# Narrow experts whose weighted rows are scattered, adding, into four sums in DRAM, in place of gathers by token

## What is computed

```python
x = x + xattn0(layernorm(x), ctx, mask)      # a0: 16 heads
x = x + ffn0(layernorm(x))                   # m0: 64 experts, top 8, 128 rows each
x = x + xattn1(layernorm(x), ctx, key_mask)  # a1: one head
x = x + local_ffn(layernorm(x))              # two layers of windowed attention
x = x + xattn2(...); x = x + ffn2(...)       # a2, m2: 8 experts, top 2
x = x + xattn3(...); x = x + ffn3(...)       # a3, m3: 8 experts, top 2
```

```python
x_buf = zeros((E * C + 1, D)).at[idx].set(x[tok])       # E=64, C=128, D=256, K=8
h = silu(einsum(xb, w_gate)) * einsum(xb, w_up)          # F=192
y = einsum(h, w_down).reshape(E * C, -1)
contrib = y[safe] * (flat_w * valid)[:, None]
routed = segment_sum(contrib, tok, num_segments=T)
return routed + silu(x @ gate_s) * (x @ up_s) @ ws_down  # the shared expert
```

## Time and profile before

| | us |
|---|---|
| median of three runs | 2786.64 |
| the profiled execution | 2789.22 |
| its span | 2787.4 |
| PE busy | 2337.7 (84%) |
| DVE busy | 1242.1 (45%) |
| ACT busy | 1077.8 (39%) |
| POOL busy | 609.0 (22%) |

### The profile page before, as it was taken

How to read it: one execution, slowest core, us unless ns; L and a number is a source line. 1 busy time by engine, 2 the same in 40 slices (tenths; PEclk the granted TensorE clock), 3 DMA queues, 4 the chain that set the end, 5 groups by cost and what they waited for, 6 DMA issues and landing times. The chain is left out here.

```text
span 2787.4 us, 44673 instructions
## 1 busy us (share of the span) xinstructions
PE 2337.7 (84%) x13238; PEld 1707.2 (61%) x13239; DVE 1242.1 (45%) x3611; ACT 1077.8 (39%) x3675; POOL 609.0 (22%) x638
## 2 busy tenths in 40 slices
PE   5998997944789989899989799379996997099991
PEld 3774786622466745566745466269984665099991
DVE  3775332435567742477733344422222564322223
ACT  2542232421356641266631355123332554044340
POOL 3277213771121210021210000310001220400004
PEclk8988898655699999999999899689998998599995
DMA  9100796333030020000000500411015101401113
GB/s 340 73 12 29 270 355 226 94 99 89 15 133 10 9 53 0 32 11 10 9 4 1 209 0 0 155 34 32 29 32 190 67 12 48 141 31 38 34 36 96
DMA packets 141735, 213.20 MB, mean 76 GB/s; under 512 B 36220, under 2 KB 110988, under 8 KB 140409
## 3 DMA queue, kind: packets, MB, share of 16 engines
q1 hardware_dynamic: 112328, 149.90, 16.3%
q0 software_dynamic: 29264, 61.54, 6.5%
HBM read 150.69 MB, written 83.52 MB: 84 GB/s over the span
## 5 line engine op out<-in xcount | busy, mean ns | idle before, releaser
L2343 POOL TENSOR_TENSOR la_invnorm<-la_clamped,all_minushalf 128x16 f32<-128x16 f32 x32 | 92.9, 2903 | 532.4 <-DVE la_clamped L2412 532.4
L826 PE MATMUL a_score_bank<-a_fold,a_xnt 128*128 (+3 forms) x448 | 183.5, 537 | 0.0
L853 PE MATMUL a_out_bank<-a_vw,a_probst 128*128 (+5 forms) x672 | 169.9, 406 | 3.6 <-ACT a_probst L762 3.4
L745 ACT ACTIVATE a_probs<-a_score_bank,a_mx 128x77 f32<-128x77 f32 x528 | 162.1, 364 | 2.7 <-DVE a_mx L640 1.7
L2070 ACT ACT_TABLE_LOAD x40 | 51.3, 1283 | 287.5 <-PE m3e_h_bank L2043 152.3
L2043 PE MATMUL m2e_h_bank<-m2e_xt,m2e_w1e 128*128 128x108 f32 x1280 | 152.2, 278 | 0.1
L2043 PE MATMUL m3e_h_bank<-m3e_xt,m3e_w1e 128*128 128x128 f32 x1280 | 152.1, 278 | 0.1
L2494 ACT ACTIVATE la_probs<-la_probs,la_nb,la_invnorm 128x256 f32<-128x256 f32 x256 | 150.1, 589 | 5.1 <-DVE la_nb L2434 5.1
L2043 PEld LDWEIGHTS m2e_h_bank<-m2e_xt,m2e_w1e 128*128 128x128 f32 x1280 | 148.8, 195 | 0.5 <-DVE m2e_xt L2084 0.4
L2043 PEld LDWEIGHTS m3e_h_bank<-m3e_xt,m3e_w1e 128*128 128x128 f32 x1280 | 148.7, 195 | 0.5 <-DVE m3e_xt L2084 0.5
L853 PEld LDWEIGHTS a_out_bank<-a_vw,a_probst 128*128 128x128 f32 (+2 forms) x672 | 129.7, 200 | 28.2 <-issue 6.8
(11 more groups left out here) (443 smaller groups left out, 4748.1 us busy)
## 6 DMA issues: line engine op xcount, KB each, us to landing
m0w_wgu<-in_m_gu SPq DMA_DIRECT2D x32, 768.0 KB, 7.2
m_xbuf<-all_zeros POOLq DMA_DIRECT2D x36, 512.0 KB, 17.9
m_w<-in_m_w SPq DMA_DIRECT2D x16, 1024.0 KB, 12.5
m0e_wd<-in_m_down SPq DMA_DIRECT2D x32, 384.0 KB, 8.0
m_xbuf<-all_zeros POOLq DMA_DIRECT2D x20, 432.0 KB, 10.1
m0w_xb<-m_xbuf SPq DMA_DIRECT2D x32, 256.0 KB, 8.4
m_ybuf<-m0e_y POOLq DMA_DIRECT2D x32, 256.0 KB, 6.3
m2w_w<-in_m_w SPq DMA_DIRECT2D x8, 1024.0 KB
```

Source lines behind the costliest of these rows:

```text
L745: last = nc.scalar.activation(probs[u][:, h * J:(h + 1) * J], score_ps[g][:, (h - h0) * J:(h - h0 + 1) * J], ACT.Exp, bias=mx[u][:, h:h + ...
L826: last = nc.tensor.matmul(score_ps[g][:, (hs[0] - h0) * J:(hs[-1] + 1 - h0) * J].rearrange("p (h j) -> p h j", j=J), xn_t[u][:, c, :], fol ...
L853: last = nc.tensor.matmul(out_ps[:, 0:D], probs_t[u][0:n, c, :], vw[0:n, bass.ds(b, 1), c, :].rearrange("p o n -> p (o n)"), start=False, ...
L2343: nc.gpsimd.tensor_tensor(inv_norm[t % 2][:, :], clamped[t % 2][:, :], k.minus_half[:, :], ALU.pow).then_inc(powered.sem, 1)
```

## The change

In a0 each row that POOL scatters into `xbuf` becomes 288 numbers wide (it was 256): behind the 256 values stand the token's eight expert numbers, its eight weights and its own number. So DVE and ACT make each tile's weights before that tile's scatter (`rank_shift`, `soften`, `carry`), and the weight work at the end of the stage goes. POOL also fills four buffers of 2560 rows in DRAM, the sums, with zeros (16 more transfers of 512 KB), and SP stores `x` with the shared expert in the first of them.

In m0 DVE finds in each pair's rows the weight and the token (`find`, `found_at`), multiplies `y` by the weight while it copies it out of PSUM, and POOL sends each expert's 128 rows by an indirect transfer that adds to the sum's rows. The two experts of a pair go to different sums, and the next pair uses the other two, so that a sum is used again two pairs later, after a wait for its last transfer (`summed`). At the end two transfers add two of the sums to the other two. The gathers and the adding on DVE go; the fold keeps its block (`fold_stage`).

`norm_scales` ahead of a1 goes, and a1's loop gets two steps more of lag: SP loads two sums' rows for each tile, DVE adds them into `x` and makes mean and variance (`combine_before`), POOL the scale (`scale_sum`). `local.load_first` stands behind SP's last load of sums.

```diff
@@ -996,12 +1031,20 @@
                 ahead.wait_scattered(sp)
                 for q in range(len(ahead.xb)):
                     ahead.load_rows(sp, q)
+                sp.wait_ge(ahead.sum_zeroed, 16 * 16)
+                for p in range(T // 2):
+                    sp.wait_ge(shared_added, p + 1)
+                    sp.dma_start(ahead.sums[0][1 + 2 * p * P:1 + 2 * (p + 1) * P, :].rearrange("(t p) d -> p t d", p=P),
+                                 k.x[:, 2 * p:2 * p + 2, :]).then_inc(ahead.x_stored, 16)
...
+                for i, total in enumerate(ahead.sums):
+                    for c in range(0 if i else SUM_ROWS // 512 - 1, SUM_ROWS // 512):
+                        pool.dma_start(total[c * 512:(c + 1) * 512, :].rearrange("(p a) d -> p (a d)", p=P), k.zeros[:, 0:4 * D]).then_inc(ahead.sum_zeroed, 16)
...
                 def scatter(t):
                     pool.wait_ge(placed, t + 1)
+                    pool.wait_ge(weighing, 2 * (t + 1))
                     for i in range(K):
...
+                def rank_shift(t):
+                    dve.wait_ge(ranked, 5 * t + 1)
+                    if t >= 2:
+                        dve.wait_ge(softened, t - 1)
+                    nc.vector.tensor_scalar(shifted[t % 2][:, :], ahead.top[:, t, 0:K], ahead.top[:, t, 0:1], None, ALU.subtract).then_inc(shifting, 1)
+
+                def carry(t):
+
+                    dve.wait_ge(softened, t + 1)
+                    nc.vector.reciprocal(sum_top[t % 2][:, :], sum_top[t % 2][:, :]).then_inc(weighing, 1)
+                    nc.vector.tensor_scalar(ahead.rows[t % R][:, IDS], idxf[t % 3][:, :], 1.0, None, ALU.add)
+                    nc.vector.tensor_copy(ahead.rows[t % R][:, TOKEN], k.token[:, t:t + 1])
+                    dve.wait_ge(weighing, 2 * t + 1)
+                    nc.vector.tensor_scalar(ahead.rows[t % R][:, WEIGHTS], exped_top[t % 2][:, :], sum_top[t % 2][:, 0:1], None, ALU.mult).then_inc(weighing, 1)
 
```

```diff
@@ -1854,6 +1915,7 @@
 
                 def load_x(q):
                     sp.wait_ge(turned, q - NX + 1)
+                    sp.wait_ge(found, 2 * (q - NX + 1))
                     r.ahead.load_rows(sp, q)
 
...
 
             @block.gpsimd
             def _(pool):
+                pool.wait_ge(r.ahead.x_stored, 16 * (T // 2))
                 for q in range(npair):
                     pool.wait_ge(y_copied, q + 1)
-                    pool.dma_start(r.ybuf[q * 2 * P:(q + 1) * 2 * P, :].rearrange("(i p) d -> p i d", p=P), y[q % 2][:, :, :]).then_inc(stored[q % 2], 16)
-                for u in range(2):
-                    pool.wait_ge(stored[u], 16 * (npair // 2))
+                    for i in range(2):
+                        j = 2 * (q % 2) + i
+                        if q >= 2:
+                            pool.wait_ge(summed[j], 16 * (q // 2))
+                        nc.gpsimd.indirect_dma_start(sums[j][:, :], bass.IndirectOffsetOnAxis(dest[q % NY][:, i:i + 1], 0), y[q % NY][:, i, :], None,
+                                                     bounds_check=SUM_ROWS - 1, oob_is_err=True, compute_op=ALU.add).then_inc(summed[j], 16)
+                for i in range(2):
+                    for j in (i, i + 2):
+                        pool.wait_ge(summed[j], 16 * (npair // 2))
+                    pool.dma_start(sums[i][1:1 + T * P, :], sums[i + 2][1:1 + T * P, :], max_dma_last_dim=4096, accum_op=ALU.add).then_inc(r.ahead.sums_joined, 16)
...
+                def find(q):
+
+                    rows = xb[q % NX]
...
+                    if q >= 1:
+                        dve.wait_ge(found, 2 * q)
+                    for i in range(2):
+                        nc.vector.scalar_tensor_tensor(picked[:, i, :], rows[:, i, IDS], float(2 * q + i + 1), rows[:, i, WEIGHTS],
+                                                       ALU.is_equal, ALU.mult)
+                    nc.vector.scalar_tensor_tensor(spot[:, :], rows[:, :, TOKEN].rearrange("p i o -> p (i o)"), 0.0, k.spare[:, :],
+                                                   ALU.is_equal, ALU.mult).then_inc(finding, 1)
+
+                def found_at(q):
+                    rows = xb[q % NX]
+                    dve.wait_ge(finding, q + 1)
+                    if q >= NY:
+                        for i in range(2):
+                            dve.wait_ge(summed[2 * (q % 2) + i], 16 * ((q - NY) // 2 + 1))
+                    nc.vector.tensor_reduce(weight[q % NY][:, :], picked[:, :, :], AX, ALU.add).then_inc(found, 1)
+                    nc.vector.tensor_tensor(dest[q % NY][:, :], spot[:, :], rows[:, :, TOKEN].rearrange("p i o -> p (i o)"), ALU.add).then_inc(found, 1)
+
                 def copy_y(q):
                     dve.wait_ge(y_made, q + 1)
-                    if q >= 2:
-                        dve.wait_ge(stored[q % 2], 16 * (q // 2))
+                    dve.wait_ge(found, 2 * (q + 1))
                     for i in range(2):
-                        last = nc.vector.tensor_copy(y[q % 2][:, i, :], y_ps[i][:, 0:D])
+                        last = nc.vector.tensor_scalar(y[q % NY][:, i, :], y_ps[i][:, 0:D], weight[q % NY][:, i:i + 1], None, ALU.mult)
                     last.then_inc(y_copied, 1)
 
                 for step in range(npair + 3):
+                    if 2 <= step < npair + 2:
+                        find(step - 2)
                     if step >= 3:
                         copy_y(step - 3)
+                    if 2 <= step < npair + 2:
+                        found_at(step - 2)
                     if 1 <= step <= npair:
                         hide(step - 1)
         r.old_sems.close()
+
```

```diff
+                if summing:
+                    sp.wait_ge(before.ahead.sums_joined, 32)
+
+                    def load_sums(t, u):
+                        sp.wait_ge(combined.sem, combined.at(t - 2, "x"))
+                        for i in range(2):
+                            sp.dma_start(got[u][:, i, :], before.ahead.sums[i][bass.ds(t * P + 1, P), :]).then_inc(gathered[u], 16)
+                    pipeline(sp, T, (0, load_sums))
                 if local:
                     local.load_first(sp)
...
+                    if summing:
+                        nc.vector.tensor_tensor(row(k.x, t), got[u][:, 0, :], got[u][:, 1, :], ALU.add).then_inc(combined.sem, 1)
+                    else:
+                        for i in range(K):
+                            if i:
+                                done("0")
+                            nc.vector.scalar_tensor_tensor(row(k.x, t), got[u][:, i, :], before.weights[:, bass.ts(t, 1), i], row(k.x, t),
+                                                           ALU.mult, ALU.add).then_inc(combined.sem, 1)
+                    done("x")
                     nc.vector.bn_stats(row(k.stats, t), row(k.x, t)).then_inc(combined.sem, 1)
                     done("stats")
                     stand_alone(dve, before_waited)
...
+            if summing:
+                @block.gpsimd
+                def _(pool):
+                    pool.sem_inc(scaled_before.sem, 2)
+
+                    def scale_sum(t, u):
+                        pool.wait_ge(combined.sem, combined.at(t, "eps"))
+                        nc.gpsimd.tensor_tensor(col(k.rstd, t), col(k.var, t), k.minus_half[:, 0:1], ALU.pow).then_inc(scaled_before.sem, 1)
+                    pipeline(pool, T, (1, scale_sum))
```

More of the change, by code:

```diff
@@ L524, in attention @@
             routed, logged = s.steps("routed"), s.steps("logged")
+        summing = before is not None and before.m is M0
         if before:
-            K = before.m.top
+            K = 2
             got, slot = s.pair("got", [P, K, D]), s.pair("slot", [P, K], U32)
@@ L532, in attention @@
             indexed, scaled_before = s.steps("indexed"), s.steps("scaledbefore")
-            combined = s.steps("combined", *(f"{i}" for i in range(K)), "stats", "copy", "aggr", "mean", "eps")
+            combined = s.steps("combined", *(("x",) if summing else ("0", "x")), "stats", "copy", "aggr", "mean", "eps")
         def later(*phases):
@@ L1031, in _ @@
                 nc.vector.memset(none3[:, :], 0.0)
+                for rows in ahead.rows:
+                    nc.vector.memset(rows[:, D:PAYLOAD], 0.0)
                 nc.vector.tensor_copy(before16[:, :], k.before[:, :])
```

106 lines of the change are left out of this document (62 added, 44 removed).

## The result

The changed kernel takes 2802.93 us (median of 4 runs, 2798.62 to 2804.36), the kernel before beside it 2786.06: a ratio of 1.0056 (95% interval 1.0038 to 1.0073), 16 to 17 us slower. The forecast was 2778.4, 8 us faster. A second comparison, later and with 6 runs, gave 2798.3 against 2786.5, 1.0042 (1.0026 to 1.0058).

What follows compares the result with a forecast made beforehand. It took PE to set m0's pair period with DMA nearly full, and gathers to set the fold stage's end. -46.2 + 21 + 8 + 5 + 2 + 2 = -8.2, giving 2778.4 against the median; range 2760 to 2822.

Steps and rivals of the forecast that it cites:

- the join: End of m0: last two scatters and two joins issued, next stage begins at about 462 in place of 459.86, +2.
- The other +2: Start of the fold: joins' traffic beside the fold's first weights, +2, up to +8 if those weights come last.
- the range's 2822: Upper end of the whole range: late sums with a landing of about 11.8 us, leaving out 1 in 10.
- Combining off the path: Fold to a1: splits start at 598.6 in place of 642.79 (44.2 us), `norm_scales` goes (2.0 us), together -46.2.
- a1: a1 takes over the adding on DVE, with more lag and late local loads: +21, bounds +17 and +36.
- m0: m0's adding scatters also read sums: 5.0 us a pair, +8, the middle between nothing and +15.5.
- a0: a0: first tile +1.8 later, SP's stores of `x` delay m0's first matmul +3.2; together +5, bounds +2 and +13.
- The late sums: Rival, m0: scatters land from 8.5 us on and delay the pairs; 2802 at 10.5 us, 2835 at 12.6; chance 0.22.
- Free adds: Rival, m0: reading the sums is free or covered by PE's period, m0's term 0: -16.2, 2770; chance 0.20.
- Blocked zeros: Rival, a0: 52 zeroing transfers too many to be outstanding, POOL's scale at 37.94 comes late, +10 to +20; chance 0.06.
- The forecast's own range: Whole kernel: 2768 to 2788 by the bounds of m0, a0 and a1; the forecast itself had 0.42.

Runs made afterwards that it cites:

- e2: Changed kernel with joins at m0's end adding only the first 1024 tokens' rows: 16.6 us from joins' first issue to next block's first load, 26.4 in c1.
- e3: Changed kernel with joins at m0's end copying in place of adding: 18.5 us from joins' first issue to next block's first load, 26.4 in c1.
- e1: Changed kernel with the joins issued by POOL at the start of the fold's block: 0.9826 times the kernel before, on the slower chip.
- e8: Changed kernel with the joins in the fold's block after the fold's weights are in, first chip: 2781.26 us, 0.9978 times the kernel before.
- e4: Changed kernel with m0's 64 scatters copying in place of adding, on the slower chip: m0 159.2 us, against 167.2 in c1.
- e11: Same kernel as e4, on the first chip: m0 157.8 us, against 157.0 in the kernel before and 165.0 in the changed kernel.
- c1: The changed kernel itself, run again on the slower chip: 2872.42 us against 2925.73 for the kernel before, 0.9803.
- e5: Changed kernel with the joins in the fold's block after the fold's weights, on the slower chip: 0.9735 times the kernel before.

## Why the prediction was wrong

**The step that failed** is the join: "the next stage begins at about 462 in place of 459.86, +2". I had the joins issued and forgotten, with a price for their traffic beside the fold's weights (+2, up to +8). The runs showed that m0's block does not end until they have landed (e2, e3 shorten them and the wait with them, e1 and e8 take both away), though the kernel's code has no wait for them there. The trace names the instruction that holds it, POOL's `DRAIN` at the block's end: 24.33 us with the joins, 14.6 and 16.5 in e2 and e3, 9.6 without them (e8), 2.67 in the kernel before. The row to the next block's load, forecast at +2, measured +27.1: about 5 for POOL's queue of scatters at the end (e8's 10.9 against 6.0, joins gone) and 22 for the joins. The other +2, for the joins' traffic beside the fold's weights, measured nothing, since the joins had landed by then (PE's first matmul comes 5.8 us after the fold's first load, 6.0 before). The upper bound did not hold it either; the range's 2822 held the time for another reason, sums that come back late, so that the time lies inside it is luck. I had read the code for the waits on `summed` and `sums_joined`, found the only reader of the latter 145 us later, and did not ask what a block's end waits for. The profile before shows POOL's last store at 454.16 and the next block at 459.86, but there the code waits for that store too, so these rows could not tell.

The Trainium skill (Collectives: The Full Stack, "The bandwidth ceiling: the fold count and why AG ≠ RS ≠ AR") says of reduce-scatter that its add needs two source reads, and puts its rate at half of a copy's. In the runs here the direction agrees and the half doesn't: the adding joins move 212 GB/s with all engines full and the copying ones (e3) 330, so an added byte takes 1.6 times as long, and in the scatters it takes 2.5 times the engines' time (32.1% for 6.15 MB against 13.9% for 6.61).

**Point by point.**

- *Combining off the path*: -46.2 forecast, -49 to -52 measured over the two rows of the table. Right, and the fold itself runs 2 to 6 us faster without the gathers beside it (133.1 to 136.4 us to its splits, where 138.7 was forecast).
- *a1*: +21 forecast, +19.1 to +19.6 measured, with DVE in steps of 4.9 us and its waits for ACT down from 9.2 to 1.6. Right, but for the lower bound: with every wait refilled it is 29.3 - 16.1 = +13, and not the +17 that stands there.
- *m0*: +8 forecast as a middle between 0 and +15.5, +8 to +9 measured. That adding costs traffic is right, and e4 and e11 show it. That the number came out is luck: the sum priced the reads of the sums as 0.26 MB at 400 GB/s, while the engines carry 340 GB/s in this stage and adding took 18 points more of their time between 320 and 440 us, 22 us; of all that m0 shows 8 us, the rest is hidden.
- *a0*: of the +5, 3.2 was to come behind the first scatter, where 5.0 to 6.2 was measured. The stores are mis-sized, 6.00 us and not 3.84, and DVE's longer loop lies under them. Ahead of the first scatter either kernel varies by 5 us, so the +1.8 is neither shown nor refuted.
- *The late sums*, the rival on the slower side, gave 2802, and the measured 2802.9 is no point for it: POOL waited 25.4 us for sums in all, but scatters land after 8.1 us, under its 8.5, and PE waited for rows, not for POOL.
- *Free adds*: refuted by e4 and e11.
- *Blocked zeros*: POOL's scale moved from 37.94, 38.01 and 38.11 to 38.83, 38.70 and 38.41, less than 1 us.
- *The forecast's own range*, 2768 to 2788, is said to be by the bounds of m0, a0 and a1. Added up, those bounds give 2763 to 2809, so its upper end was drawn too low by the prediction's own terms.

Taking the failed step out gives the forecast back: with the joins under the fold (e8) the kernel is 5.3 us faster than before, where 8 was predicted. In part that is by errors that cancel: the scatters queued at m0's end (+5) and a0 (+2) against the faster fold.

**What stays open.** On the other chip the changed kernel is 2% faster than the kernel before (c1), and e5 2.7% faster. There a0 takes 59 to 79 us longer in the changed kernel (241.5 to 261.5 us from the first scatter, against 182.6), with engines waiting for issue up to 12.6 us at a time, while its stages from m0 to a1's start repeat those of the first chip within 3 us. The kernel before loses 139 us there. a0 and the stage of gathers are both long code that runs once or nearly so, so the removed stage may be where the kernel before loses. That is only argued: no profile of the kernel before came from that chip.

## What to carry to other kernels

A transfer with no reader nearby can still be waited for, here at the end of the block in which POOL issued it: ask what the block's end waits for, and put such a transfer into the block whose work can cover it, behind the loads that this block needs first. Moving it only to the block's start (e1) turned a wait of 22 us into a fold that was 22 us longer, 15 of them ahead of its first matmul, for late weights. Look in the trace for the `DRAIN` of each block's end as well. And price an accumulating transfer by engine time, not by its bytes: here 1.6 times that of a copied byte from DRAM to DRAM, and 2.5 times in the indirect form.

## What the hardware showed that I had not expected

- A block's end waited for POOL's transfers to land, in a `DRAIN` on POOL: 24.3 us, 14.6 with half of the bytes, 16.5 with the same bytes copied, 9.6 with only scatters to wait for (e8; POOL was still issuing them for 5 of these), 2.67 with nothing.
- Adding in a transfer: 212 GB/s DRAM to DRAM with all 16 engines busy, where copying moves 330; the indirect form takes 1.55 us of POOL for each 128 rows, where the copying form takes 0.98, and 6744 packets in place of 2422 between 320 and 440 us.
- The same two programs compare as 1.0056 and 1.0042 where the kernel before takes 2786 us and as 0.980 on another chip, on which the kernel before is 5% slower and the changed one 2.5%: a verdict of half a per cent holds for chips like the one on which it was taken.
